# A fused residual chain on one core: the stage 1 weight buffers are placed behind the working buffers in SBUF

## The reference

```python
x = x + _L0_cond_ref(x, ...)   # causal EMA, gated; three 512x512 products and one 512x1024
x = x + _L1_cond_ref(x, ids, W, b)            # x @ W[id] + b[id]
x = x + _L2_cond_ref(x, ids, W1, b1, W2, ...) # 512 -> 128 -> 512 adapter, residual, layer norm
x = x + _L3_cond_ref(x, ids, weight, bias)    # x @ weight[id].T + bias[id]
```

## Time and profile before

| | us |
|---|---|
| median of 3 runs (lowest, highest) | 746.0 (745.98, 746.4) |
| span of the profiled execution, first to last instruction | 744.8 |
| PE busy in it | 734.5 |
| DVE, ACT, POOL busy in it | 539.0, 372.5, 121.4 |
| granted TensorE clock, mean | 0.998 |

### The profile page before, as it was taken

One profiled execution on the slowest core, in us unless ns is written; L12 is line 12 of the kernel. 1 busy time (PEld: TensorE's weight loads), 2 busy tenths in 40 slices (PEclk: granted clock), 3 DMA queues, 4 the chain that ended last, 5 costly groups with the idle time before them and its releaser, 6 DMA issues.

```text
span 744.8 us, 10092 instructions
## 1 busy us (share of the span) xinstructions
PE 734.5 (99%) x3317; PEld 596.3 (80%) x3317; DVE 539.0 (72%) x808; ACT 372.5 (50%) x554; POOL 121.4 (16%) x220
## 2 busy tenths in 40 slices
PE   9999999999999999999999999999998999999998
PEld 7778888888888788888788887888786878888886
DVE  5798895695695596597587578876977586677573
ACT  4375455446435535535545543747557375563530
POOL 2000030030022003004004024105301022021110
PEclk9999999999999999999999999999999999999999
DMA  7989208916934953962970971642642626433312
GB/s 197 258 124 179 50 1 129 180 59 102 191 74 83 189 95 56 194 116 45 181 141 12 158 226 57 226 152 106 214 116 91 174 85 194 99 132 96 85 71 84
DMA packets 119310, 93.54 MB, mean 126 GB/s; under 512 B 75583, under 2 KB 103262, under 8 KB 117230
## 3 DMA queue, kind: packets, MB, share of 16 engines
q1 hardware_dynamic: 116174, 88.13, 52.5%
q10 hardware_dynamic: 2912, 5.01, 2.2%
q0 software_dynamic: 192, 0.00, 0.1%
HBM read 32.28 MB, written 25.20 MB: 77 GB/s over the span
## 4 chain that ended last, share of the span: by engine, by line
PE 87%; DVE 6%; issue 2%; SPq 1%; DMA 1%; ACT 1%; ACTq 0%; POOL 0%; DVEq 0%; POOLq 0%
PE pc L690 11%; PE pc L689 11%; PE pc L688 11%; PE pt L688 7%; PE pt L690 7%; PE pt L689 7%; PE pm L690 5%; PE pm L688 5%; PE pm L689 5%; PE pm L808 4%; PE pm L806 4%; PE pm L807 4%; PE pm L695 2%; SPq L307 1%; PE pt L695 1%
## 5 line engine op out<-in xcount | busy, mean ns | idle before, releaser
L688 PE MATMUL pc<-x_h,wg_h 128*128 128x512 f32 x224 | 88.8, 396 | 3.1 <-DVE s_l L1770 3.0
L690 PE MATMUL pc<-x_h,wg_l 128*128 128x512 f32 x224 | 88.5, 395 | 0.0
L689 PE MATMUL pc<-x_l,wg_h 128*128 128x512 f32 x224 | 88.3, 394 | 0.0
L1569 DVE TENSOR_TENSOR_SCAN stage_b<-alpha,carry,stage_b 128x512 f32<-128x512 f32 x64 | 78.7, 1271 | 0.0
L688 PEld LDWEIGHTS pc<-x_h,wg_h 128*128 128x128 f32 x224 | 42.4, 189 | 13.9 <-ACT soma L1338 3.4
L806 PE MATMUL pm<-t_h,wt_h 128*128 128x512 f32 x128 | 50.4, 394 | 0.5 <-DVE t_l L1582 0.5
L1201 ACT ACTIVATE ctx_t<-ctx_t,col_all 128x512 f32<-128x512 f32 x32 | 23.1, 723 | 55.3 <-DVE ctx_t L1549 55.3
L688 PE MATMUL pm<-wo_h,s_h 128*128 128x512 f32 x128 | 50.7, 396 | 0.0
L808 PE MATMUL pm<-t_h,wt_l 128*128 128x512 f32 x128 | 50.6, 395 | 0.0
L690 PE MATMUL pm<-wo_h,s_l 128*128 128x512 f32 x128 | 50.5, 395 | 0.0
L689 PE MATMUL pm<-wo_l,s_h 128*128 128x512 f32 x128 | 50.5, 395 | 0.0
(11 more groups left out here) (280 smaller groups left out, 1884.3 us busy)
## 6 DMA issues: line engine op xcount, KB each, us to landing
x_planes<-x_pairs SPq DMA_DIRECT2D x56, 256.0 KB, 7.3
xt_scratch<-x_t SPq DMA_DIRECT2D x8, 1024.0 KB, 10.4
n_scratch<-stage_a SPq DMA_DIRECT2D x8, 1024.0 KB, 10.0
ctx_t<-xt_scratch SPq DMA_DIRECT2D x16, 512.0 KB, 7.0
x_pairs<-n_scratch SPq DMA_DIRECT2D x14, 512.0 KB, 5.9
out_dram<-x_tok SPq DMA_DIRECT2D x28, 256.0 KB, 2.3
x_planes<-stage_b SPq DMA_DIRECT2D x84, 64.0 KB, 2.0
mod<-mod_scratch ACTq DMA_DIRECT2D x8, 512.0 KB, 3.7
```

The source lines that it names most:

```text
L688: nc.tensor.matmul(acc, ah, bh, start=start and q == 0, stop=False)
L689: nc.tensor.matmul(acc, ah, bl, start=False, stop=False)
L690: last = nc.tensor.matmul(acc, al, bh, start=False, stop=stop and q == n - 1)
L1569: nc.vector.tensor_tensor_scan(tr[:, m % 2, :], alpha[:, 1 + d:2 + d].to_broadcast([P, BLK]), tr[:, m % 2, :], carry[:, D - d, m:m + 1], A ...
```

## The change

The twelve weight tensors, six lines, are declared after `ident` instead of ahead of `x_tok`. No instruction, wait, DMA or order differs; only addresses do.

```diff
-
-        wg_h, wg_l = sb("wg_h", [P, 2 * NC, E], F32R), sb("wg_l", [P, 2 * NC, E], F32R)
-        ws_h, ws_l = sb("ws_h", [P, NC, E], F32R), sb("ws_l", [P, NC, E], F32R)
-        wt_h, wt_l = sb("wt_h", [P, NC, E], F32R), sb("wt_l", [P, NC, E], F32R)
-        wo_h, wo_l = sb("wo_h", [P, NC, E], F32R), sb("wo_l", [P, NC, E], F32R)
-        wn1_h, wn1_l = sb("wn1_h", [P, NC, H], F32R), sb("wn1_l", [P, NC, H], F32R)
-        wn2_h, wn2_l = sb("wn2_h", [P, D], F32R), sb("wn2_l", [P, D], F32R)

         x_tok = sb("x_tok", [P, 2, E])
...
         ident = sb("ident", [P, P])
+
+        wg_h, wg_l = sb("wg_h", [P, 2 * NC, E], F32R), sb("wg_l", [P, 2 * NC, E], F32R)
+        ws_h, ws_l = sb("ws_h", [P, NC, E], F32R), sb("ws_l", [P, NC, E], F32R)
+        wt_h, wt_l = sb("wt_h", [P, NC, E], F32R), sb("wt_l", [P, NC, E], F32R)
+        wo_h, wo_l = sb("wo_h", [P, NC, E], F32R), sb("wo_l", [P, NC, E], F32R)
+        wn1_h, wn1_l = sb("wn1_h", [P, NC, H], F32R), sb("wn1_l", [P, NC, H], F32R)
+        wn2_h, wn2_l = sb("wn2_h", [P, D], F32R), sb("wn2_l", [P, D], F32R)
```

## The result

| | before | after |
|---|---|---|
| median, us (runs; lowest, highest) | 746.2 (4; 745.98, 749.53) | 737.55 (4; 736.94, 738.58) |
| ratio after / before, 95% interval | | 0.9868 [0.9844, 0.9892] |
| span of the profiled execution, us | 744.8 | 735.2 |
| pace of the 512-column matmuls, ns, weight stationary / data stationary | 230.3 / 233.3 | 227.0 / 227.2 |

The paces in the last line are means over the steps from one start to the next between 512-column matmuls in the trace, some 2090 and 792 of them in each kernel, with steps over 300 ns left out.

The account below looks back on a forecast made before the run. The prediction took the kernel to be bound by the pace of TensorE's matmul stream. Its matmul, DMA and other-engine terms were each 0, so the forecast stayed at the median, 746.0 us, range 740.3 to 752.0.

Parts of the forecast that it names:

- Matmuls* term: Stages 1 and 2: matmul cost lies between all at 229.0 ns (5.7 us less) and all at 233.3 (6.7 more); 0 taken.
- The faster rival: All matmuls: equal alignment lets the fast pace hold everywhere, 740.3 us in full, range 740.3 to 744.5; chance 0.33.
- Which bits: Buffer starts: weights at multiples of 128 bytes, working buffers 64 past; the change puts both at multiples of 128; no separate size.
- The slower rival: 2136 weight-stationary matmuls: moving operands starting at multiples of 128 go slow, 752.7 us in full, range 747.5 to 752.7; chance 0.30.
- The reading of the two paces: Stage 1, temp_product: same code at 233.3 and 229.0 ns; neither clock, traffic nor addresses alone decide, the preceding stream's state seems to.
- The weight load: Around mod_product: two-column loads take 0.08 us, not 0.19, yet matmuls stay 230 ns apart; speaks against an effect through loads.
- DMAs and other engines: Two DMA legs on the chain: 1.0 us either way, 0 taken; other engines' instructions, with VectorE under TensorE: 0 taken.
- The clock step: Stage 2, after the 3.0 us wait: a shorter or longer wait could gain or lose about 1 us; only widens the range.

Follow-up runs that it names:

- experiment 3: After's order with weights alone 64 bytes up (weights at 192, data at 128 modulo 256): 750.63 us, ratio 1.0031 to before.
- experiment 9: Before's order with data 192 bytes up, so weights and data both start at 128 modulo 256: 737.17 us, ratio 0.9865 to before.
- experiment 12: After's order with weights 192 bytes up, so data start 64 bytes past the weights as in before: 746.54 us, ratio 0.9981 to before.
- Experiment 1: Before's order with data 64 bytes up (weights at 128, data at 0 modulo 256): 751.79 us, ratio 1.0034 to before.
- experiment 5: After's order with weights 256 bytes up, at 128 again modulo 256: 736.21 us, ratio 0.9836 to before.
- experiment 2: After's order with everything 64 bytes up (weights and data both at 192 modulo 256): 737.59 us, ratio 0.9881 to before.
- experiment 10: After's order with everything 128 bytes up (weights and data both at 0 modulo 256): 736.98 us, ratio 0.9857 to before.
- experiment 4: Before's order with wo and wn1 at 192, the weights wg, ws, wt at 128 and data at 0 modulo 256: 750.77 us, ratio 1.004 to before.
- experiment 8: After's order with wg_l alone 64 bytes up: 740.89 us, ratio 0.9902 to before.
- experiment 11: After's order with x_l alone 64 bytes up: 743.86 us, ratio 0.9946 to before.

## Why the prediction was wrong

**The step that failed** is the bound of the *Matmuls* term: "The cost is bounded by the two paces", 229.0 and 233.3 ns, and between these ends 0 was taken. Equal starts make a third pace, 226.7 ns, outside both ends. The prediction had said that no row shows a matmul with equal low bits, and its last sentence named a third pace as what would make it wrong; it still bounded the unseen case by the paces of unequal starts. With 226.7 ns in its own arithmetic a block takes 255 x 0.2267 = 57.81 us, 1.08 less than its mean of 58.89, 8.6 us in eight blocks; stage 2 gains 384 x (233.8 - 226.7 ns) + 480 x (229.4 - 226.7 ns) = 4.0 us. That is 12.6 us, of which 9.6 arrived in the span. Of the 3.0 that are missing, the first 63 us account for some 1.3 (the running difference stands at +0.25 there, where a block's gain of 1.08 was counted), and TensorE's waits for 1.2 (8.1 against 6.9 us). The rest is not assigned. Neither this sum nor the prediction's counts the 96 matmuls of xx_product.

**The faster rival had the right mechanism** and a wrong size. "The slow pace came from operands 64 bytes apart" held, in that the distance between the two operands decides (experiments 3, 9, 12), and the slow blocks did vanish with it. Its 740.3 took the pace of before's better blocks as the best there is. That pace, too, was one of operands out of step.

**Which bits.** That weights and data were 64 bytes off by their low bits was read rightly from the addresses, but "a multiple of 128" was the wrong measure. Experiment 1 refuted it, experiment 5 put the period at 256 bytes, and after's buffers happen to agree within 256.

**The slower rival**, that the moving operand's own start decides, is refuted by experiments 2 and 10: 64 and 128 bytes more on every operand change nothing.

**The reading of the two paces** was right in that neither clock nor traffic makes them, and that addresses alone do not choose between 229.0 and 233.3 ns. What was missed is that this choice was seen at one distance only: where the moving operand starts 64 bytes past the stationary one (before, experiments 4 and 12, and l3_tile in 3). A pace is also a mean: in the stretch of 229.0 ns from 170.23 us the steps after L806, L807 and L808 average 225.6, 229.4 and 231.6 ns, and in the out_product from 148.03 us steps of about 231 and 236 ns alternate. Single steps as short as those of after were thus in the trace of before, under a mean that was taken for a bound. So the row that was called nearest, one code at two paces on unchanged addresses, was the wrong guide to a placement that has no such choice.

**The weight load.** That a load of two columns does not shorten the matmul beside it stands, but it weighed nothing against an effect of placement: in experiment 8 the cost is mostly with the pair whose own two operands disagree. The Trainium skill (TensorE: Matmul & The Clock Gate, "Step-by-step: what each phase is for") has two independent read ports for the two operands; the inference drawn from it, that no placement changes a matmul, does not hold here: 226.7 against 233.3 ns for the same code. The measurement decides.

**DMAs and other engines** were taken at 0, and nothing contradicts it: common starts at 0, 128 and 192 give 736.98, 737.55 and 737.59 us with overlapping intervals. By the page on DMA: Bandwidth & Descriptors in the Trainium skill ("How a descriptor splits into AXI transactions") a start of the data at 0 would have read in fewer beats than one at 192; no run shows it in the time.

**The clock step** stands behind the long wait in both kernels. It costs about 1.6 us in before, where eight matmuls from 569.18 take 3.40 us, and 1.4 in after, where seven from 591.28 take 3.02. That is somewhat more than the 1 us or so that the prediction gave it, and only the difference of some 0.2 us is in the result.

## What to carry to other kernels

When a kernel is a stream of float32r matmuls, look at the start addresses of both operands modulo 256 and let them agree, for the high and the low parts alike; one pad of 192 bytes was worth 1.3% here, and any later edit of the buffer list can undo it. A pace that differs between two pieces of the same code at full clock is a reason to look at addresses, and the better of two paces seen is no bound for a placement that has not been seen. Bring a rule of thumb on alignment to the chip at several distances before it is believed: 32, 64, 128, 192 and 224 bytes were all worse, and only 0 and 256 were good.

## What the runs showed of the hardware

I had not expected that a matmul of 128 by 128 by 512 in float32r, at a granted clock of 1.00 (2.4 GHz), would have average paces that depend on the distance between its operands' starts: 226.7 ns at 0 or 256 bytes, about 233 on average where the moving operand starts 32, 128, 192 or 224 bytes past the stationary one, and either 229.0 or 233.3 where it starts 64 past. That a pair out of step sits among pairs in step costs about 9 ns on itself and 1 to 2 on its neighbours when the stationary operand is the one that is off (experiment 8), and about 5 ns on each of three when it is the moving one (experiment 11).

Three things stay open. Why equal starts help is not shown by any run, and only float32r with 512 columns was tried. What chooses between the two paces at 64 bytes is unknown, beyond that one of them can hold through several products, as the slow one does through soma_chunk and temp_product in the earlier trace rows. And why the longer of the two waits for s_l is the second one in after, where it was the first, was not tried.
